# A four-layer graph network on one core: the scatter of the edges by node in small portions

## The reference, cut to what matters

```python
x = x + L0_gnn(layernorm(x), src, dst, edge_weight)   # relu((A @ x) @ W), A from the edges
x = x + L0_ffn(layernorm(x))      # top 2 of 16 experts, then an affine layer norm
x = x + L1_gnn(layernorm(x), ...) # x @ W_self + (A @ x) @ W_neigh + bias
x = x + L1_ffn(layernorm(x))      # top 2 of 8 experts
x = x + L2_gnn(layernorm(x), src, dst, ...)   # attention over the edges, grouped by dst
x = x + L2_ffn(layernorm(x))
x = x + L3_gnn(layernorm(x), ...) # three products with A, batch norms
x = x + L3_ffn(layernorm(x))
```

## Time and profile before

| | us |
|---|---|
| timed, median of 3 runs | 6410.36 (6409.36 to 6415.48) |
| profiled execution: span from the first to the last instruction | 7555.1 |
| profiled execution: time around the span | none is given |
| PE busy in the profile | 5066.7 (67% of the span) |
| DVE busy | 2842.8 (38%) |
| POOL busy | 2221.8 (29%) |
| ACT busy | 1117.7 (15%) |
| columns to `dst_table`, 392 indirect DMAs, POOL busy | 380.0 |
| columns to `bin_table`, 392 indirect DMAs, POOL busy | 402.3 |
| matmuls of the five products (L1173), PE busy | 1443.9, with 397.6 idle before them |

### The profile page before, as it was taken

How to read it: one execution, slowest core, us unless ns; L and a number is a source line. 1 busy time by engine, 2 the same in 40 slices (tenths; PEclk the granted TensorE clock), 3 DMA queues, 4 the chain that set the end, 5 groups by cost and what they waited for, 6 DMA issues and landing times. The chain is left out here.

```text
span 7555.1 us, 86117 instructions
## 1 busy us (share of the span) xinstructions
PE 5066.7 (67%) x21628; PEld 3356.8 (44%) x21677; DVE 2842.8 (38%) x6162; ACT 1117.7 (15%) x2691; POOL 2221.8 (29%) x2417
## 2 busy tenths in 40 slices
PE   3511969659783597755454965554877969898954
PEld 2410547314771256733222843222767844444433
DVE  4260679201323004244445944445943220202052
ACT  2210235000220002210000120000123220101020
POOL 3356010540244401425553215553300410000014
PEclk9999999769796697977776976777988989999966
DMA  0000023223561223637774827675721644243323
GB/s 14 1 1 1 1 93 139 81 66 120 160 199 65 77 90 123 195 122 228 219 218 137 273 86 224 216 222 160 254 67 40 191 153 153 101 139 115 115 69 114
DMA packets 484296, 952.76 MB, mean 126 GB/s; under 512 B 112617, under 2 KB 292436, under 8 KB 481686
## 3 DMA queue, kind: packets, MB, share of 16 engines
q1 hardware_dynamic: 324614, 633.98, 24.9%
q0 software_dynamic: 114208, 281.05, 12.8%
q10 hardware_dynamic: 45296, 35.56, 1.6%
HBM read 733.91 MB, written 216.46 MB: 126 GB/s over the span
## 5 line engine op out<-in xcount | busy, mean ns | idle before, releaser
L1173 PE MATMUL banks<-ring,xn 128*128 128x512 f32 (+1 forms) x3500 | 1443.9, 568 | 397.6 <-issue 276.9
L1173 PEld LDWEIGHTS banks<-ring,xn 128*128 128x128 f32 x3500 | 644.2, 195 | 1198.0 <-issue 1181.4
L1909 PE MATMUL banks<-agg,hotT 128*128 x1664 | 687.0, 519 | 633.6 <-issue 623.9
L1000 POOL DMA_INDIRECT rows<-pairs,idxr x832 | 804.7, 967 | 640.5 <-DVE scores L1888 373.2
L1909 PEld LDWEIGHTS banks<-agg,hotT 128*128 128x128 f32 x1664 | 319.7, 237 | 949.2 <-issue 945.1
L382 POOL DMA_INDIRECT dst_table<-nodes_pay,nodes_row x392 | 380.0, 969 | 817.5 <-DVEq L1147 478.9
L382 POOL DMA_INDIRECT bin_table<-bins_pay,bins_row x392 | 402.3, 1026 | 592.1 <-ACTq L783 206.8
L1882 DVE TENSOR_TENSOR prod<-banks,rows 128x512 f32<-128x512 f32 x416 | 267.9, 686 | 811.3 <-PE banks L1909 640.7
L1643 PE MATMUL banks<-second,hT 128*128 x1544 | 391.6, 393 | 45.4 <-DVE yr L1689 19.3
L1628 PE MATMUL banks<-xT,w1r 128*128 128x128 f32 x3088 | 403.1, 283 | 12.3 <-DVE xT L1681 7.1
L2162 PE MATMUL banks<-msg,hot 128*128 128x264 f32 x1664 | 384.3, 392 | 16.7 <-DVE msg L2132 16.2
(11 more groups left out here) (355 smaller groups left out, 6931.4 us busy)
## 6 DMA issues: line engine op xcount, KB each, us to landing
ring<-adjacency SPq DMA_DIRECT2D x145, 1280.0 KB
spill<-rows SPq DMA_DIRECT2D x208, 512.0 KB
rows<-spill SPq DMA_DIRECT2D x208, 512.0 KB
w1r<-in_L_ffn_W SPq DMA_DIRECT2D x114, 512.0 KB
adjacency<-strips SPq DMA_DIRECT2D x13, 3200.0 KB
w1r<-in_L_ffn_w SPq DMA_DIRECT2D x65, 512.0 KB
rows<-home_rows SPq DMA_DIRECT2D x35, 640.0 KB
ring<-adjacency SPq DMA_DIRECT2D x25, 640.0 KB
```

What stands on the lines that cost most here:

```text
L1000: nc.gpsimd.indirect_dma_start(rows[:, row, :], None, table, bass.IndirectOffsetOnAxis(ap=idxr[:, at + g:at + g + 1], axis=0))\
L1173: last = nc.tensor.matmul(K.ps[2 * (g % 2) + o][:, 0:wd], x[:, t * D + o * P:t * D + (o + 1) * P], ring.buffer[:, n % R, 0:wd // cols, q * ...
L1909: last = nc.tensor.matmul(K.ps[2 + 2 * (jj % 2) + g // 2][:, g % 2 * D:(g % 2 + 1) * D], hotT[:, jj % 2, g * P:(g + 1) * P], tile_of(q, t) ...
```

## The change

`Scatter.paced` is new. It takes a semaphore that counts finished portions of the stage's work, and sends `count` columns at the start and then `count` more for each portion that is finished. `spmm`, `project` and `dense` now hand their semaphore and its number of portions to the `beside` function; `dense` and `combine` get such a function at all. The 392 columns are spread over eight stages: 140 beside the product of layer 0 (four per slice of 35), 10 beside its projection, 25 beside the router's dense of layer 0 (one per tile), 12 beside its combine, 28 beside its affine layer norm, 140 beside the product of layer 1, 25 beside its projection (one per tile), and the last 12 beside the router's dense of layer 1, where `finish` now stands.

```diff
@@ class Scatter
+    def paced(self, pool, passed, marks, count):
+
+        for n in range(marks):
+            if n:
+                pool.wait_ge(passed, n)
+            self.columns(pool, min(count, COLS - self.next))
@@ def spmm
                 if beside:
-                    beside(pool)
+                    beside(pool, used, GROUPS * slices)
@@ def dense
-def dense(nc, K, sources, weights, bias, outs, norm=None, ahead=None):
+def dense(nc, K, sources, weights, bias, outs, norm=None, ahead=None, beside=None):
...
                 if ahead:
                     ahead.clear()
+                if beside:
+                    beside(pool, written, NT)
@@ def combine
-def combine(nc, K, picks, weights, first, dst, relu=False):
+def combine(nc, K, picks, weights, first, dst, relu=False, beside=None):
...
+            @block.gpsimd
+            def _(pool):
+                if beside:
+                    beside(pool)
@@ def moe
-        route(nc, K, r, gate, experts, picks, mode, ahead)
+        route(nc, K, r, gate, experts, picks, mode, ahead, beside[0])
...
-            combine(nc, K, picks, r.weights, K.xn, K.agg)
-            layer_norm(nc, K, K.agg, K.agg, affine=after, residual=True)
+            combine(nc, K, picks, r.weights, K.xn, K.agg, beside=beside[1])
+            layer_norm(nc, K, K.agg, K.agg, affine=after, residual=True, beside=beside[2])
@@ def layer0_gnn
-    project(nc, K, K.agg, [A["L0_gnn_weight"]], None, None, None)
+    project(nc, K, K.agg, [A["L0_gnn_weight"]], None, None, beside[3])
@@ def build
-        beside = [lambda pool: of_nodes.columns(pool, COLS // 2), lambda pool: of_nodes.columns(pool, COLS - COLS // 2 - 16),
-                  of_nodes.finish]
+        beside_slices = lambda pool, used, slices: of_nodes.paced(pool, used, slices, 4)
+        beside_moe = (lambda pool, written, tiles: of_nodes.paced(pool, written, tiles, 1),
+                      lambda pool: of_nodes.columns(pool, 12), lambda pool: of_nodes.columns(pool, 28))
+        beside_tiles = lambda pool, written, tiles: of_nodes.paced(pool, written, tiles, 1)
+
+        def last_tiles(pool, written, tiles):
+            of_nodes.paced(pool, written, tiles, 1)
+            of_nodes.finish(pool)
+
+        beside = [beside_slices, beside_slices, beside_tiles, lambda pool, written, tiles: of_nodes.columns(pool, 10)]
...
-                        2, "softmax_of_top", ACT.Relu, after=(A["L0_ffn_gamma"], A["L0_ffn_beta"])),
+                        2, "softmax_of_top", ACT.Relu, after=(A["L0_ffn_gamma"], A["L0_ffn_beta"]), beside=beside_moe),
...
-                        2, None, ACT.Gelu),
+                        2, None, ACT.Gelu, beside=(last_tiles, None, None)),
```

More of the change, by code:

```diff
@@ L1733, in _, with route @@
                         ins.then_inc(added, 1)
-def route(nc, K, r, gate, experts, picks, mode, ahead):
+def route(nc, K, r, gate, experts, picks, mode, ahead, beside):
     gate_w, gate_b = gate
@@ L1747, in route @@
         found_i = big.sb("found_i", [P, NT], I32)
-        dense(nc, K, [K.x], [[gate_w]], gate_b, [(experts, "sb", logits, None)], norm=(K.xn, K.table), ahead=ahead)
+        dense(nc, K, [K.x], [[gate_w]], gate_b, [(experts, "sb", logits, None)], norm=(K.xn, K.table), ahead=ahead, beside=beside)
         with stage(nc) as st:
@@ L1816, in route, with moe @@
         items_of_slots(nc, K, lane[:, :], chunk[:, :], token[:, :], r.home[:, :], r.idx[:, :])
-def moe(nc, K, gate, w1, b1, w2, b2, picks, mode, func, relu_out=False, after=None):
+def moe(nc, K, gate, w1, b1, w2, b2, picks, mode, func, relu_out=False, after=None, beside=(None, None, None)):
     experts = w1.shape[0]
```

## The result

| timed, median | kernel before | changed kernel | ratio |
|---|---|---|---|
| the runs that the forecast is held against | 6412.92 (6409.36 to 6417.15, 4 runs) | 6459.22 (6453.42 to 6462.83, 4 runs) | 1.0073 (1.006 to 1.0085) |
| later, on a chip of another kind | 7551.83 (7543.59 to 7578.42, 7 runs) | 7232.59 (7219.02 to 7255.73, 4 runs) | 0.9578 (0.9547 to 0.9609) |

What follows compares the result with a forecast made beforehand. TensorE was taken to bound both products at some 269 us each in timed runs, hiding GpSimd's columns. Costs 0.5 + 1 + 21 = +22.5 us on 6410.4 gave 6433 us timed, range 6388 to 6446.

Steps and rivals of the forecast that it cites:

- The products: Both products: four columns, 5.1 us, stay hidden under a slice of 8.6 us; timed gain 0, at most 172 us.
- Rival (c): Products: late GpSimd makes columns back to back again, profile keeps its stall; 6410 to 6422 us; 28% together with (b).
- The stall: TensorE's unnamed 1.79 us pauses, 378 us over both products, belong to the profiled execution and are absent from timed runs.
- rival (a): Products: the stall is partly real in timed runs, so thinning gains time; 6238 to 6397 us, chance 22%.
- The affine layer norm: 28 columns there: one held until VectorE's 75 operations end, 16 left to send; +21 us, between 0 and +25.
- Rival (b): Affine layer norm: GpSimd passes between VectorE's operations, 0 to +10 us; 6410 to 6422 us, 28% together with (c).
- The first router's dense: Layer 0 router: 24 paced columns end with the last stored tile; +0.5 us, between 0 and 2.
- Combine, both projections, second router's dense: Combine: four last columns slip into VectorE's DMA pauses or end behind the stage, +1 us, 0 to 5; the others 0 each.

Runs made afterwards that it cites:

- 28 slices: Changed kernel with five columns after each of a product's first 28 slices instead of four after each of 35: 6422.17 us against 6411.17 for the kernel before.
- one column per short slice: Changed kernel with five, four and, in the last group's slices, one column per slice: 7193.63 us against 7544.22; on the first kind 6425.78 against 6411.73.
- two others: 28 columns beside the affine layer norm: changed kernel with 28 slices paced, 6422.17 us; kernel before with only those columns moved there, 6421.23 us.
- three passes: Kernel before with 28 columns moved beside the affine layer norm, its 75 operations in three passes of 25, waits only between passes: stage 54.7 us.

## Why the prediction was wrong in size

- **The products, the step that failed.** "Four columns are 5.1 us against a slice of 42.91 / 5 = 8.6 us, still hidden" holds for 30 slices of 35. The last group has 128 columns, and its slices take 11.16 / 5 = 2.2 us. Both numbers stood in the earlier trace rows and in the first paragraph. 17.8 + 18.2 = 36 of the 46 us are this, put at 0 in the sum; the experiments with 28 slices and with one column per short slice take it away. Rival (c) had the mechanism, GpSimd late against the count and its columns back to back, but I priced it at nothing.
- **The stall.** Its account was near: I had 335 us in the ranking, 440 in attention and 378 in the products, together 1153. Between the two profiles of the kernel before they are 353, 386 and 372, and 28 in the last routed stage. That 1153 met the gap of 1145 so closely is in part luck, since the single terms are off by up to 54 us and cancel. What followed from it was half right. The timed runs shown were indeed free of it, so the gain there was 0. But it does not belong to a profiled execution: on the second kind of chip the timed runs are as long as the profiled one, the changed kernel is 319 us faster, and rival (a)'s premise holds. The span forecast for the changed kernel beside a span of 7555, about 7200, was 7224.6 there. One profile and timed runs of one program could not tell chip from execution; that took a second chip.
- **The affine layer norm.** +21 was forecast, the changed kernel paid 6.1, 9.8 to 12.2 in two others. I carried the 14.03 us of a run of scalar_tensor_tensor over to a run with a tensor_tensor in every third place. In three passes the held columns of 8 us appear, each pass of scalar_tensor_tensor with one. Rival (b) was nearer, and its bound of 10 us was about right.
- **The first router's dense.** +0.5 forecast, +3.4 measured. GpSimd's last column ends at 1384.42 and its first operation in the next block starts at 1387.35, 2.93 us later: I had reckoned when the columns end, and nothing for the end of the block behind them.
- **Combine, both projections, second router's dense.** Forecast +1, 0, 0 and 0; they came to +0.2, 0, -0.9 and 0. In the combine the columns took 1.01 to 1.14 us though all operations there are scalar_tensor_tensor from SBUF; there every second one starts 0.52 us behind the one before it instead of 0.40, which leaves 0.04 us without an operation. The held column that ended between two passes, at 0.03 us without one, fits that a gap lets it in; no experiment put gaps into a run to test it, and the 14.03 us with waits between had none.
- **The sum.** The misses had opposite signs: 36 + 3 too little, 15 + 2 too much, 6433 + 22 = 6455; the kernel before was 2.5 us slower beside the changed one than in the runs shown, which makes 6457.5 against 6459. A range that held only the known terms was too narrow, because a term taken as 0 had no bound on its far side. That the direction came out right is in part luck: 21 of the 22.5 us forecast stood in the layer norm, which paid 6.1, and 36 of the 46 measured lie where the forecast had nothing.

## What to carry to other kernels

Before work is handed out per portion, compare its length with the shortest portion, not the mean one: the last portions of a loop have nobody behind them to hide a backlog. Work that issues DMAs from GpSimd must end some microseconds before its block does. When a profiled span stands far from the timed median, take the profile again on another chip before deciding whose the difference is: here 1145 us went with the chip, and the same change is +0.7% on one kind and -4.2% on the other.

## What the runs showed of the hardware

- Chips differ: the same program takes 6411 us on three and 7550 on two, repeatably (19 and 9 timed runs of one program within 0.4%). Nearly all of the difference lies where GpSimd issues indirect DMAs without a pause. TensorE then does a matmul of 1.01 us every 2.80 us; GpSimd's own pace is the same on both, 1.27 us per column. In the products a pause of 1.25 us after six columns removes it. It sets in after 34 or 35 columns beside matmuls of 0.43 us and after eight beside those of 0.11, 92 to 97 and 85 matmuls after the row began. What the engines wait for in it no view names.
- VectorE and an indirect DMA of GpSimd: a run of scalar_tensor_tensor from SBUF without gaps held one column for 8.0 and 8.4 us (25 operations) and 14.03 or 15.37 (50), with or without semaphore waits between that cost no time; it ended 0.84 to 0.85 us behind the end of the run. Beside 25 tensor_tensor of 128x256 in fp32 a column took 1.04.
- A block ends 2.9 to 5.2 us behind the end of GpSimd's last column when that comes from a row of columns, and 9.2 behind a single one (two runs, GpSimd idle for 26 and 219 us before it), against 1.0 us behind ScalarE's last copy.
